# Graph convolution of one core's kernel: the gathered messages split into three bf16 parts, and a 0/1 one-hot in place of the weighted fp32 one

## The chip, the core and the metric

The kernel runs on one core of a Trainium2 chip. The metric is the device time of one launch in microseconds (us); the median of three runs before the change is 5700.91 us (5697.95 to 5701.5). Engines are named as in the profile: PE is TensorE's matmul, PEld its weight load, DVE VectorE, ACT ScalarE, POOL GpSimd, SP SyncE.

## The reference

The program is a chain of nine stages on a node matrix `x` of 625 nodes by 512 features; each stage works on a layer-normed `x` and most add their output to it. 20000 directed edges (`src`, `dst`, `edge_weight`), sorted by `dst`, join the nodes. The change touches the fourth stage alone, the graph convolution:

```python
deg  = segment_sum(w, dst_f) + self loops;  dinv = where(deg > 0, rsqrt(deg), 0)
h    = x @ W_conv                                        # 625 x 128
agg  = segment_sum(h[src_f] * (dinv[src_f] * w * dinv[dst_f])[:, None], dst_f) + b_conv
out  = agg @ W_lin + b_lin                               # 625 x 512
```

All of it is fp32.

## The kernel before

`program` runs the stages one after the other, each in a block of its own: no engine begins a stage before all have left the one before, apart from the layer norm between them, which is a block too. So a stage's length adds to the launch's time as it is.

The stage `gcn` has the functions of five queues. Edges lie as 125 partitions by 160 columns (R = 125, ET = 160); step k takes column k, so each step handles 125 edges and there are 160 steps. In the loops one lap is 16 steps (SLOTS).

- SP loads the weights; after DVE has scaled `h` by `dinv`, it stores `h` to HBM as `gcn_h_rows` (L528).
- POOL issues one indirect DMA per step (L538), which gathers 125 rows of 128 fp32 from `gcn_h_rows` into slot `rows[:, i]` of 16. Before every fourth gather it waits for `idx_ready`, which DVE signals.
- DVE makes, per step, the weighted one-hot `hot` of 125 x 625 fp32 (L561: compare `iota_f` with `dstf`, times `w`), two buffers deep; it first waits until PE has finished with the buffer (`hot_used`). On every fourth step it copies the next four columns of indices (L575), eight steps ahead.
- PE waits for the gather and for the one-hot and multiplies: `rows` as stationary operand, `hot` as moving one, 500 columns into bank 0 (L616) and 125 into bank 1 (L618), all 160 steps accumulated in PSUM. An fp32 product shows as two MATMUL records.
- ACT takes one square root (L595) and does nothing in the loop.

After the loop PE closes the banks (L621), DVE copies them out (L579, L580), and PE multiplies by `W_lin` (L625 to L629).

Nothing orders the loop but these semaphores. Three other stages are of use for reading prices: the edge count before it (L198 to L227: one-hots of 125 x 625 bf16 made from the fp16 iota, and bf16 products of 512 and 116 columns); the relational sum (L1080 gathers, L1133 index copies, L1135 one-hots in fp16, L1162 the upper part on ACT, L1138 the lower part on DVE, both 512 wide, L1179 products); and the split ahead of the LSTM (L1397, L1323, L1401, L1328: ACT, DVE, ACT, DVE, 512 wide, from PSUM).

Of the kernel before, what the change touches and what calls it, by code (L numbers as in the profile page):

```python
# [6 lines left out]
F32 = mybir.dt.float32  # L7
F16 = mybir.dt.float16
BF16 = mybir.dt.bfloat16
U32 = mybir.dt.uint32  # L10
I32 = mybir.dt.int32
ACT = mybir.ActivationFunctionType
# [3 lines left out]
N = 625  # L16
D = 512
R = 125
# [3 lines left out]
ET = E // R  # L22
# [456 lines left out]
SLOTS = 16  # L479
# [4 lines left out]
def gcn(nc, ctx, B):  # L484

    I = B.I
    H = I["L1_gnn_W_conv"].shape[1]

    def sb(name, shape, dt):
        return here.enter_context(nc.sbuf_tensor(name, shape, dt))  # L490

    def sem(name):
        return nc.alloc_semaphore(name)

    (loaded, deg_step, root_done, rsqrt_step, h_done, h_scaled, h_stored, idx_kept, hot_ready,
     hot_used, agg_done, agg_kept, bias_ready, bias_done, out_done) = [sem("gcn_" + n) for n in (
         "loaded deg_step root_done rsqrt_step h_done h_scaled h_stored idx_kept hot_ready "
         "hot_used agg_done agg_kept bias_ready bias_done out_done").split()]
    gathered = [sem(f"gcn_gathered{i}") for i in range(SLOTS)]
    idx_ready = [sem(f"gcn_idx_ready{i}") for i in range(SLOTS // LOT)]  # L500
    h_dram = nc.dram_tensor("gcn_h_rows", (N, H), F32, kind="Internal").ap()
# [1 line left out]
    with ExitStack() as here:  # L503
# [10 lines left out]
        idx_all = sb("gcn_idx_all", [R, ET + AHEAD * LOT], I32)  # L514
        idx = sb("gcn_idx", [R, SLOTS], I32)
        rows = sb("gcn_rows", [R, SLOTS, H], F32)
        hot = sb("gcn_hot", [R, 2, N], F32)
        aggT = sb("gcn_aggT", [H, N], F32)
        block = here.enter_context(nc.Block())

        @block.sync
        def _(sp):
            sp.dma_start(wc[:], I["L1_gnn_W_conv"].rearrange("(c p) h -> p c h", p=128)).then_inc(loaded, 16)
            sp.dma_start(wl[:], I["L1_gnn_W_lin"]).then_inc(loaded, 16)
            sp.dma_start(bc[:], I["L1_gnn_b_conv"].rearrange("(h a) -> h a", a=1)).then_inc(loaded, 16)
            sp.dma_start(bl[:], I["L1_gnn_b_lin"].rearrange("(a d) -> a d", a=1)).then_inc(loaded, 16)
            sp.wait_ge(h_scaled, NT)
            sp.dma_start(h_dram.rearrange("(j p) h -> p j h", p=R), h[:]).then_inc(h_stored, 16)  # L528
# [14 lines left out]
        @block.vector  # L543
        def _(dve):
            nc.vector.memset(idx_all[:, ET:ET + AHEAD * LOT], 0).then_inc(idx_kept, 1)
            nc.vector.tensor_copy(idx_all[:, 0:ET], B.srci[:]).then_inc(idx_kept, 1)
            nc.vector.tensor_scalar(deg[:], B.wdeg[:], 1.0, None, ALU.add).then_inc(deg_step, 1)
            dve.wait_ge(deg_step, 1)
            nc.vector.tensor_scalar(has[:], deg[:], 0.0, None, ALU.is_gt).then_inc(deg_step, 1)
            nc.vector.tensor_scalar(deg[:], deg[:], 1e-30, None, ALU.max).then_inc(deg_step, 1)  # L550
            dve.wait_ge(root_done, 1)
            inverse_root(nc, dve, dinv[:], deg[:], root[:], rsqrt_step, 0)
            nc.vector.tensor_tensor(dinv[:], dinv[:], has[:], ALU.mult).then_inc(deg_step, 1)
            dve.wait_ge(deg_step, 4)
            for m in range(NT):
                dve.wait_ge(h_done, m + 1)
                nc.vector.tensor_scalar(h[:, m, :], B.bank[2 + m][0:R, 0:H], dinv[:, m:m + 1], None,
                                        ALU.mult).then_inc(h_scaled, 1)

            def hots(k, b):  # L560
                nc.vector.tensor_scalar(hot[:, b, :], B.iota_f[:], B.dstf[:, bass.ds(k, 1)],  # L561
                                        B.w[:, bass.ds(k, 1)], ALU.is_equal, ALU.mult).then_inc(hot_ready, 1)

            dve.wait_ge(idx_kept, 2)
            for i in range(AHEAD):
                nc.vector.tensor_copy(idx[:, i * LOT:(i + 1) * LOT], idx_all[:, i * LOT:(i + 1) * LOT]
                                      ).then_inc(idx_ready[i], 1)
            with dve.Fori(0, ET // SLOTS) as g:
                for i in range(SLOTS):
                    k = g * SLOTS + i  # L570
                    dve.wait_ge(hot_used, k + 1)
                    if i % LOT == 0:

                        at = (i + AHEAD * LOT) % SLOTS
                        nc.vector.tensor_copy(idx[:, at:at + LOT], idx_all[:, bass.ds(k + AHEAD * LOT, LOT)]  # L575
                                              ).then_inc(idx_ready[at // LOT], 1)
                    hots(k, i % 2)
            dve.wait_ge(agg_done, 1)
            nc.vector.tensor_copy(aggT[:, 0:500], B.bank[0][0:H, 0:500]).then_inc(agg_kept, 1)  # L579
            nc.vector.tensor_copy(aggT[:, 500:N], B.bank[1][0:H, 0:R]).then_inc(agg_kept, 1)  # L580
            nc.vector.tensor_scalar(bc_wide[:], B.ones[0:H, 0:R], bc[:, 0:1], None, ALU.mult).then_inc(bias_ready, 1)
            for m in range(NT):
                dve.wait_ge(out_done, m + 1)
                nc.vector.scalar_tensor_tensor(out=B.x[:, m, :], in0=B.bank[2 + m][0:R, :],
                                               scalar=dinv[:, m:m + 1], in1=B.x[:, m, :], op0=ALU.mult,
                                               op1=ALU.add).then_inc(deg_step, 1)
            dve.wait_ge(bias_done, 1)
            dve.wait_ge(deg_step, 4 + NT)
            for m in range(NT):
                nc.vector.tensor_tensor(B.x[:, m, :], B.x[:, m, :], B.bank[7][0:R, :], ALU.add)  # L590

        @block.scalar
        def _(act):
            act.wait_ge(deg_step, 3)
            nc.scalar.activation(root[:], deg[:], ACT.Sqrt).then_inc(root_done, 1)  # L595

        @block.tensor
        def _(pe):
            pe.wait_ge(loaded, 64)
            for m in range(NT):  # L600
                for c in range(KC):
                    last = nc.tensor.matmul(B.bank[2 + m][0:R, 0:H], xnT[:, c, m * R:(m + 1) * R], wc[:, c, :],
                                            start=(c == 0), stop=(c == KC - 1))
                last.then_inc(h_done, 1)
            for i in range(2):
                last = nc.tensor.matmul(B.bank[i][0:H, :], B.zero[:, 0:H], B.zero[:], start=True, stop=False)
            last.then_inc(hot_used, 2)
            pe.wait_ge(h_scaled, NT)
            for m in range(NT):
                o = B.bank[0][0:H, m * R:(m + 1) * R] if m < 4 else B.bank[1][0:H, 0:R]  # L610
                nc.tensor.matmul(o, h[:, m, :], B.ident[0:R, 0:R], start=False, stop=False)
            with pe.Fori(0, ET // SLOTS) as g:
                for i in range(SLOTS):
                    pe.wait_ge(gathered[i], (g + 1) * 16)
                    pe.wait_ge(hot_ready, g * SLOTS + i + 1)
                    nc.tensor.matmul(B.bank[0][0:H, 0:500], rows[:, i, :], hot[:, i % 2, 0:500], start=False,  # L616
                                     stop=False)
                    nc.tensor.matmul(B.bank[1][0:H, 0:R], rows[:, i, :], hot[:, i % 2, 500:N], start=False,  # L618
                                     stop=False).then_inc(hot_used, 1)
            for i in range(2):  # L620
                last = nc.tensor.matmul(B.bank[i][0:H, :], B.zero[:, 0:H], B.zero[:], start=False, stop=True)  # L621
            last.then_inc(agg_done, 1)
            pe.wait_ge(agg_kept, 2)
            for m in range(NT):
                nc.tensor.matmul(B.bank[2 + m][0:R, :], aggT[:, m * R:(m + 1) * R], wl[:], start=True, stop=True  # L625
                                 ).then_inc(out_done, 1)
            pe.wait_ge(bias_ready, 1)
            nc.tensor.matmul(B.bank[7][0:R, :], bc_wide[:], wl[:], start=True, stop=False)
            nc.tensor.matmul(B.bank[7][0:R, :], B.ones[0:1, 0:R], bl[:], start=False, stop=True  # L629
                             ).then_inc(bias_done, 1)  # L630
# [1839 lines left out]
```

## Time and profile before

| what | value |
|---|---|
| median of 3 runs | 5700.91 us (5697.95 to 5701.5) |
| the profiled execution's own time | 5706.91 us |
| its span, first to last instruction | 5705.1 us |
| mean granted TensorE clock | 0.954 |
| PE busy | 5027.5 us (88%) |
| DVE busy | 2837.5 us (50%) |
| ACT busy | 1437.0 us (25%) |
| POOL busy | 633.6 us (11%) |
| the gcn loop, first gather to last product | 657.3 to 911.8 us |

Busy shares are an average over nine stages with different limits; for this change only the stretch from 657 to 920 us counts. Times in rows are us from the start of the span, or ns where a group's mean is given. A step's place in the loop is best read from the gathers, of which there is exactly one per step.

### The profile page before, as it was taken

The page shows a single profiled execution, that of the slowest core. Times are in us where ns is not written, and L with a number is a line of the kernel's source. Part 1 is how long each engine was busy: PE and PEld are TensorE (multiplying, and loading weights), DVE is VectorE, ACT ScalarE, POOL GpSimd, SP SyncE. Part 2 cuts the span into 40 slices and gives each one's busy share as a digit, 9 for nine tenths or more (in the row PEclk, how much of TensorE's full clock was granted, in tenths as well). Part 3 has the DMA queues.
Part 4 walks back from the last instruction along what each step waited for, and adds up shares of the span by engine and source line. Part 5 has one row for each costly group of instructions (what it writes and reads, how often), then busy time and mean ns, then how long its engine had stood idle before and what let it go on. Part 6 is the DMA issues. An engine that isn't in the chain of part 4 may idle for free. (4 is left out here: it accounts for less than half of the span.)

```text
span 5705.1 us, 267215 instructions
## 1 busy us (share of the span) xinstructions
PE 5027.5 (88%) x109528; PEld 3080.5 (54%) x109528; DVE 2837.5 (50%) x11506; ACT 1437.0 (25%) x4745; POOL 633.6 (11%) x1073
## 2 busy tenths in 40 slices
PE   8899686899998989999999999999999999777688
PEld 6644343444565446666666666666666666554444
DVE  4501344232554755555555555555555555574533
ACT  0000000012332343333333333333333333242222
POOL 0000382000662110000000000000000000021000
PEclk9899897999999989999999999999999999898877
DMA  0000111166444740000000000000000000000200
GB/s 11 15 30 15 30 42 31 56 240 240 125 120 144 258 129 12 10 10 12 10 10 10 12 10 10 12 11 10 10 12 10 10 12 10 19 15 36 74 12 9
DMA packets 157671, 265.00 MB, mean 46 GB/s; under 512 B 48686, under 2 KB 83636, under 8 KB 153241
## 3 DMA queue, kind: packets, MB, share of 16 engines
q1 hardware_dynamic: 102548, 181.63, 9.6%
q0 software_dynamic: 55040, 82.30, 5.1%
q8 instruction: 47, 0.77, 0.1%
q14 instruction: 36, 0.29, 0.0%
HBM read 178.38 MB, written 85.14 MB: 46 GB/s over the span
## 5 line engine op out<-in xcount | busy, mean ns | idle before, releaser
L1558 PE MATMUL bank<-lstm_w,step_h_parts 128*32 128x128 f16 x87360 | 1453.8, 220 | 241.8 <-issue 241.8
L1558 PEld LDWEIGHTS bank<-lstm_w,step_h_parts 128*32 128x32 f16 x87360 | 1238.4, 97 | 613.3 <-issue 349.3
L1629 DVE TRANSPOSE_TENSOR_REDUCE step_summed<-bank 128x4 f32 (+1 forms) x2500 | 792.4, 317 | 1085.2 <-PE bank L1558 914.5
L1553 PE MATMUL bank<-step_xg,step_rows 128*128 (+1 forms) x2500 | 757.7, 385 | 45.1 <-DMA step_xg<-lstm_xg 18.8
L1526 ACT ACTIVATE step_act_out<-step_summed,lstm_inv_scale 128x4 f32<-128x4 f32 x625 | 185.8, 297 | 1724.1 <-DVE step_summed L1629 1724.1
L1514 POOL COPY xnT<-step_state 128x4 f32 (+1 forms) x625 | 116.7, 187 | 2759.9 <-DVE step_state L1654 2759.9
L1179 PE MATMUL bank<-sum_parts,sum_hot 125*125 125x512 f16 x1600 | 346.9, 380 | 6.7 <-DVE sum_parts L1138 6.7
L1179 PEld LDWEIGHTS bank<-sum_parts,sum_hot 125*125 125x125 f16 x1600 | 219.0, 137 | 135.0 <-DVE sum_parts L1138 7.5
L1429 PE MATMUL bank<-xg_w,xnT 128*125 128x512 f32 x640 | 276.6, 595 | 6.7 <-DMA xg_w<-in_c_w_ih 6.7
L538 POOL DMA_INDIRECT gcn_rows<-gcn_h_rows,gcn_idx x160 | 202.5, 1265 | 703.3 <-issue 703.3
L1553 PEld LDWEIGHTS bank<-step_xg,step_rows 128*128 128x128 bf16 x2500 | 142.5, 97 | 167.7 <-issue 129.8
L1080 POOL DMA_INDIRECT sum_rows<-rel_h,sum_idx x160 | 211.7, 1323 | 118.0 <-DVE sum_idx L1133 80.0
L226 PE MATMUL bank<-cnt_hot_s,cnt_hot_d 125*125 125x512 bf16 x800 | 221.5, 387 | 3.4 <-DVE cnt_hot_s L202 3.4
L616 PE MATMUL bank<-gcn_hot,gcn_rows 125*128 125x500 f32 x320 | 177.7, 637 | 47.3 <-DMA gcn_rows<-gcn_h_rows,gcn_idx 44.5
L1588 PE MATMUL bank<-lstm_wsel,step_state 128*1 128x4 f32 x4992 | 215.0, 168 | 4.3
L1585 PEld LDWEIGHTS bank<-step_input_score,ones 1*1 1x1 f32 x1248 | 65.5, 75 | 281.8 <-issue 281.8
L1592 PE MATMUL bank<-step_h_weight,step_tc 128*1 128x4 f32 x4992 | 214.1, 168 | 0.0
L1532 ACT ACTIVATE step_act_out<-step_summed,lstm_inv_scale 128x4 f32<-128x4 f32 x625 | 185.9, 297 | 96.4 <-DVE step_summed L1629 26.0
L1429 PEld LDWEIGHTS bank<-xg_w,xnT 128*125 128x125 f32 x640 | 120.7, 189 | 162.1 <-issue 154.8
L143 ACT ACTIVATE ln_root<-ln_var_sb 125x5 f32<-125x5 f32 x8 | 1.7, 208 | 817.3 <-DVE ln_var_sb L124 817.3
L1529 ACT ACTIVATE step_act_out<-step_summed,lstm_inv_scale 128x4 f32<-128x4 f32 x625 | 185.8, 297 | 76.2 <-DVE step_summed L1629 16.6
L1537 ACT ACTIVATE step_act_out<-step_summed,lstm_inv_scale 128x4 f32<-128x4 f32 x625 | 185.9, 297 | 42.8 <-DVE step_summed L1629 1.5
(370 smaller groups left out, 6369.6 us busy)
## 6 DMA issues: line engine op xcount, KB each, us to landing
rel_h<-rel_h_sb SPq DMA_DIRECT2D x39, 1024.0 KB, 6.4
lstm_xg<-cnt POOLq DMA_DIRECT2D x80, 375.0 KB, 3.7
step_xg<-lstm_xg SPq DMA_DIRECT2D x375, 80.0 KB
xg_w<-in_c_w_ih SPq DMA_DIRECT2D x16, 1024.0 KB
lstm_w<-in_c_w_hh SPq DMA_DIRECT2D x16, 1024.0 KB, 11.6
cheb_w<-in_L_gnn_weight SPq DMA_DIRECT2D x8, 1024.0 KB
choose_we<-in_L_ffn_experts SPq DMA_DIRECT2D x8, 1024.0 KB
rel_bases<-in_L_gnn_bases SPq DMA_DIRECT2D x8, 1024.0 KB, 11.4
```

Source lines behind the costliest of these rows:

```text
L226: nc.tensor.matmul(B.bank[m][0:R, :], hd, hot_s[:, b, 0:512], start=False, stop=False)
L538: nc.gpsimd.indirect_dma_start(out=rows[:, i, :], out_offset=None, in_=h_dram, in_offset=bass.IndirectOffsetOnAxis(ap=idx[:, i:i + 1], axis=0)
L1080: nc.gpsimd.indirect_dma_start(out=rows[:, i, :], out_offset=None, in_=B.rel_h, in_offset=bass.IndirectOffsetOnAxis(ap=idx[:, i:i + 1], ax ...
L1179: last = nc.tensor.matmul(B.bank[m][0:R, :], hot[:, i % BUFS, m * R:(m + 1) * R], parts[:, i % BUFS, a, :], start=False, stop=False)
L1429: last = nc.tensor.matmul(B.bank[i % 6][0:R, :], xnT[:, c, m * R:(m + 1) * R], w[:, n % 2, c, :], start=(c == 0), stop=(c == KC - 1))
L1532: nc.scalar.activation(act_out[:, 8:12], summed[:, 8:12], ACT.Sigmoid, scale=L.inv[:, 0:1]).then_inc(sig_i, 1)
L1537: nc.scalar.activation(act_out[:, 12:16], summed[:, 12:16], ACT.Sigmoid, scale=L.inv[:, 0:1]).then_inc(sig_o, 1)
L1553: return nc.tensor.matmul(bank[:], rows[:, p, :], xg[:, at, :], start=True, stop=stop)
L1558: last = nc.tensor.matmul(bank[32 * q:32 * q + 32, 128 * s:128 * s + 128], h_parts[:, c, :], w[:, s, c, q, a, 128 * p:128 * p + 128], star ...
L1588: nc.tensor.matmul(score[:, 0:CELLS], state[:, k:k + 1], L.wsel[:, :, k], start=False, stop=False)
L1592: last = nc.tensor.matmul(score[:, 0:CELLS], tc[:, k:k + 1], h_weight[:, :, k], start=False, stop=(k == KC - 1))
L1629: nc.vector.tensor_reduce(summed[:, 4 * p:4 * p + 4], bank[:, bass.ds(s * 128, 128)].rearrange("p (b r) -> p b r", r=32), X_AXIS, ALU.add, ...
```

## The change

Each gathered message is multiplied by its edge weight and split into three bf16 numbers whose sum is the fp32 product: `hi` (ACT, bf16 of `w * row`), `rest` (DVE, `w * row - hi`, fp32), `mid` (ACT, bf16 of `rest`), `lo` (DVE, `rest - mid`, bf16). The one-hot holds only 0 and 1, in bf16, and comes from the fp16 iota. PE multiplies the three parts with the same one-hot: six bf16 products per step. The rings `hot`, `rest` and `parts` are four deep (`hot` was two deep), and PE waits for DVE's `hot_ready` and `lo_ready`; the wait for the gather moves from PE to ACT. POOL's and SP's programs stay as they are.

```diff
-        hot = sb("gcn_hot", [R, 2, N], F32)
+        hot = sb("gcn_hot", [R, 4, N], BF16)
+        rest = sb("gcn_rest", [R, 4, H], F32)
+        parts = sb("gcn_parts", [R, 4, 3, H], BF16)
...
-            def hots(k, b):
-                nc.vector.tensor_scalar(hot[:, b, :], B.iota_f[:], B.dstf[:, bass.ds(k, 1)],
-                                        B.w[:, bass.ds(k, 1)], ALU.is_equal, ALU.mult).then_inc(hot_ready, 1)
+            def split_rows(k, i):
+                dve.wait_ge(hi_ready, k + 1)
+                nc.vector.scalar_tensor_tensor(out=rest[:, i % 4, :], in0=rows[:, i, :], scalar=B.w[:, bass.ds(k, 1)],
+                                               in1=parts[:, i % 4, 0, :], op0=ALU.mult, op1=ALU.subtract
+                                               ).then_inc(rest_ready, 1)
+                nc.vector.tensor_scalar(hot[:, i % 4, :], B.iota_h[:], B.dstf[:, bass.ds(k, 1)], None,
+                                        ALU.is_equal).then_inc(hot_ready, 1)
+                dve.wait_ge(mid_ready, k + 1)
+                nc.vector.tensor_tensor(parts[:, i % 4, 2, :], rest[:, i % 4, :], parts[:, i % 4, 1, :], ALU.subtract
+                                        ).then_inc(lo_ready, 1)
...
-                    k = g * SLOTS + i
+                    k = dve.snap(g * SLOTS + i)
                     dve.wait_ge(hot_used, k + 1)
...
-                    hots(k, i % 2)
+                    split_rows(k, i)
...
             nc.scalar.activation(root[:], deg[:], ACT.Sqrt).then_inc(root_done, 1)
+            with act.Fori(0, ET // SLOTS) as g:
+                for i in range(SLOTS):
+                    k = act.snap(g * SLOTS + i)
+                    free = act.snap(k + 1)
+                    due = act.snap((g + 1) * 16)
+                    act.wait_ge(hot_used, free)
+                    act.wait_ge(gathered[i], due)
+                    nc.scalar.activation(parts[:, i % 4, 0, :], rows[:, i, :], ACT.Copy, scale=B.w[:, bass.ds(k, 1)]
+                                         ).then_inc(hi_ready, 1)
+                    act.wait_ge(rest_ready, free)
+                    nc.scalar.copy(parts[:, i % 4, 1, :], rest[:, i % 4, :]).then_inc(mid_ready, 1)
...
-            last.then_inc(hot_used, 2)
+            last.then_inc(hot_used, 4)
...
-                    pe.wait_ge(gathered[i], (g + 1) * 16)
                     pe.wait_ge(hot_ready, g * SLOTS + i + 1)
-                    nc.tensor.matmul(B.bank[0][0:H, 0:500], rows[:, i, :], hot[:, i % 2, 0:500], start=False,
-                                     stop=False)
-                    nc.tensor.matmul(B.bank[1][0:H, 0:R], rows[:, i, :], hot[:, i % 2, 500:N], start=False,
-                                     stop=False).then_inc(hot_used, 1)
+                    pe.wait_ge(lo_ready, g * SLOTS + i + 1)
+                    for a in range(3):
+                        nc.tensor.matmul(B.bank[0][0:H, 0:500], parts[:, i % 4, a, :], hot[:, i % 4, 0:500],
+                                         start=False, stop=False)
+                        last = nc.tensor.matmul(B.bank[1][0:H, 0:R], parts[:, i % 4, a, :], hot[:, i % 4, 500:N],
+                                                start=False, stop=False)
+                    last.then_inc(hot_used, 1)
```

## Rows read from the trace of the kernel before

**Rows 1.** Who waited for whom, 661 to 912 us: total us, times, longest
```profile
POOL gcn_rows L538 <- issue: 48.2, 158, 0.3
PE bank L616 <- DMA gcn_rows<-gcn_h_rows,gcn_idx: 44.5, 119, 8.6
```
**Rows 2.** Timeline, POOL's second gather and the last: start, duration, idle before
```profile
659.10 1.21 POOL L538 DMA_INDIRECT gcn_rows<-gcn_h_rows,gcn_idx  x1 [0.30 <-issue]
...
906.97 1.22 POOL L538 DMA_INDIRECT gcn_rows<-gcn_h_rows,gcn_idx  x1 [0.30 <-issue]
```
**Rows 3.** Timeline of PE, the loop's last product and the work behind it
```profile
910.52 1.10 PE L616 MATMUL bank<-gcn_hot,gcn_rows 125*128 125x500 f32 x2 [0.34 <-DMA gcn_rows<-gcn_h_rows,gcn_idx]
911.68 0.60 PE L621 MATMUL bank<-zero 128*128 128x512 bf16 x2
913.25 4.56 PE L625 MATMUL bank<-gcn_wl,gcn_aggT 128*125 128x512 f32 x10 [0.97 <-DVE gcn_aggT L580]
```
**Rows 4.** Timeline, POOL's gathers between 740 and 748 us
```profile
740.55 1.21 POOL L538 DMA_INDIRECT gcn_rows<-gcn_h_rows,gcn_idx  x1 [0.30 <-issue]
746.76 1.40 POOL L538 DMA_INDIRECT gcn_rows<-gcn_h_rows,gcn_idx  x1 [0.30 <-issue]
```
**Rows 5.** Timeline, DVE's one-hots beside the gathers of rows 4
```profile
741.15 0.89 DVE L561 TENSOR_SCALAR gcn_hot<-iota_f,dstf,w 125x625 f32<-125x625 f32 x1
747.20 0.61 DVE L561 TENSOR_SCALAR gcn_hot<-iota_f,dstf,w 125x625 f32<-125x625 f32 x1
```
**Rows 6.** Groups by line and shape, edge count, 20 to 242 us: busy us, mean ns
```profile
L226 PE MATMUL bank<-cnt_hot_s,cnt_hot_d 125*125 125x512 bf16 x800 | 221.5, 387 | 3.4 <-DVE cnt_hot_s L202 3.4
L198 DVE TENSOR_SCALAR cnt_hot_d<-iota_h,dstf 125x625 bf16<-125x625 f16 x159 | 61.5, 387 | 99.6 <-PE bank L227 99.6
```
**Rows 7.** Groups by line and shape, whole span, ACT and DVE: mean ns
```profile
L1162 ACT ACTIVATE sum_parts<-sum_rows,sum_norm 125x512 f16<-125x512 f32 x160 | 115.5, 722 | 243.1 <-PE bank L1179 219.5 <-DMA sum_rows<-rel_h,sum_idx 22.1 <-issue 1.4
L1535 ACT COPY step_input_score<-xn 1x4 f32 x622 | 109.6, 176 | 0.0
L1401 ACT CAST cnt<-xn 125x512 bf16<-125x512 f32 x80 | 49.1, 614 | 6.6 <-DVE xn L1323 6.4
L1932 ACT ACTIVATE gat_out<-gat_res 125x256 f32<-125x256 f32 x40 | 16.8, 419 | 7.2 <-DVE gat_res L2001 7.2
L2001 DVE SCALAR_TENSOR_TENSOR gat_res<-bank,gat_inv,gat_bias 125x256 f32<-125x256 f32 x40 | 19.4, 484 | 13.8 <-PE bank L1880 12.7
L1739 DVE SCALAR_TENSOR_TENSOR x<-bank,x 125x128 f32<-125x128 f32 x20 | 4.4, 284 | 1.8 <-PE bank L1729 1.7
```
**Rows 8.** Timeline of the relational sum, ACT's upper part and DVE's lower
```profile
1506.38 0.72 ACT L1162 ACTIVATE sum_parts<-sum_rows,sum_norm 125x512 f16<-125x512 f32 x1 [1.44 <-PE bank L1179]
1507.22 0.75 DVE L1138 SCALAR_TENSOR_TENSOR sum_parts<-sum_rows,sum_norm,sum_parts 125x512 f16<-125x512 f32 x1 [0.45 <-ACT sum_parts L1162]
```
**Rows 9.** Timeline of the relational sum: two gathers and the DVE work within them
```profile
1436.54 1.21 POOL L1080 DMA_INDIRECT sum_rows<-rel_h,sum_idx  x1 [0.30 <-issue]
1463.40 1.29 POOL L1080 DMA_INDIRECT sum_rows<-rel_h,sum_idx  x1 [0.30 <-issue]
...
1436.95 0.75 DVE L1138 SCALAR_TENSOR_TENSOR sum_parts<-sum_rows,sum_norm,sum_parts 125x512 f16<-125x512 f32 x1 [4.11 <-ACT sum_parts L1162]
1437.61 0.38 DVE L1135 TENSOR_SCALAR sum_hot<-iota_h,dstf 125x625 f16<-125x625 f16 x1
1463.23 0.39 DVE L1135 TENSOR_SCALAR sum_hot<-iota_h,dstf 125x625 f16<-125x625 f16 x1 [0.58 <-PE bank L1179]
```
**Rows 10.** Timeline of PE at the lower clock, edge count: successive products of one kind
```profile
21.25 0.64 PE L226 MATMUL bank<-cnt_hot_s,cnt_hot_d 125*125 125x512 bf16 x1
21.79 0.64 PE L226 MATMUL bank<-cnt_hot_s,cnt_hot_d 125*125 125x512 bf16 x1
```
**Rows 11.** Stretches: busy us (count) of each engine, then granted clock, DMA share, GB/s
```profile
946.00:997.00 51.00, 21.06 (x53) 11.35 (x54) 30.23 (x88) 0.00 (x0) 0.00 (x0) 0.60 0.00 0
661.00:911.70 250.70, 211.89 (x641) 109.32 (x642) 110.03 (x197) 0.00 (x0) 199.34 (x158) 0.99 0.17 41
```

More of the change, by code:

```diff
@@ L493, in sem @@
         return nc.alloc_semaphore(name)
[L495 to L498, printed above, removed]
+    (loaded, deg_step, root_done, rsqrt_step, h_done, h_scaled, h_stored, idx_kept, hi_ready, rest_ready,
+     mid_ready, lo_ready, hot_ready, hot_used, agg_done, agg_kept, bias_ready, bias_done, out_done) = [sem("gcn_" + n) for n in (
+         "loaded deg_step root_done rsqrt_step h_done h_scaled h_stored idx_kept hi_ready rest_ready "
+         "mid_ready lo_ready hot_ready hot_used agg_done agg_kept bias_ready bias_done out_done").split()]
     gathered = [sem(f"gcn_gathered{i}") for i in range(SLOTS)]
```

## The prediction

> **What bounds the kernel now.** The stages do not overlap, so the change is worth what it takes off or adds to the gcn stage, and the first question is who paces its loop. I read the waits of that stretch first, then POOL's and DVE's timelines side by side. The waits [rows 1] point away from PE: it waits 119 times of 160 for a gather that has not landed, 44.5 us in all. POOL is the only engine that waits for no other: before each of its 158 gathers there stand 0.3 us of its own issue and nothing else. The gathers run from 659.10 to 906.97 us, 158 of them [rows 2]: 247.87 / 158 = 1.569 us a step. A step of PE, by the stretch [rows 11], is 211.89 us / 160 = 1.32 us, so PE has 0.25 us spare per step. POOL's gather stream is the bound, and the fp32 products that the change replaces are not.
>
> The second reading is why a gather takes 1.21 us in one row and 1.40 in another [rows 4]. Laid beside DVE's one-hot [rows 5], with the phase counted from the gather's start: a one-hot that starts at 0.44 (747.20 - 746.76) lasts 0.61, ends at 1.05 and the gather takes 1.40, which is that end plus 0.35. One that starts at 0.60 (741.15 - 740.55) lasts 0.89 instead of 0.61, and the gather stays at 1.21. So the two engines exclude each other for a short part of the gather: whoever is late waits. By the first pair the gather suffers from a one-hot that has begun before it and ends after 1.21 - 0.35 = 0.86; by the second, a later one suffers itself, and the border between the two lies between 0.44 and 0.60. An undisturbed gather costs 1.21 + 0.30 = 1.515 us; the mean of 1.569 holds 0.054 us of this contention.
>
> **The change part by part.**
>
> *PE.* It loses two fp32 products a step and gets three pairs of bf16 ones, 500 and 125 columns. The edge count runs the same kind of pair (512 and 116 columns): 221.5 us of unbroken work over 800 pairs [rows 6] = 0.277 us a pair, so 0.83 us a step at the full clock. PE falls from 1.32 to 0.83 us and stays off the path; the gain of 0.49 us a step is worth nothing inside the loop, since the step before already waited for the gather.
>
> *ACT.* Two operations of 128 columns a step, none of which the trace has. For `hi` I take the line through a tiny copy (0.176) and L1162's 512 columns (0.722) [rows 7], which at 128 gives 0.31; I take 0.33, and the upper bound is the 256-column row, 0.42, the lower the tiny copy, 0.18. `mid` is a cast: between 0.176 and L1401's 0.614 the line gives 0.29, with bounds 0.18 and 0.42.
>
> *DVE.* `rest` and `lo` have two tensor inputs and 128 columns: 0.28 each by L1739; L2001 with 256 columns bounds it above at 0.48 [rows 7], and 0.18 below. The one-hot shrinks from 0.60 to 0.387 us [rows 6]. The index copies stay. DVE does 0.28 + 0.39 + 0.28 = 0.95 us a step, and the index copies that it has now.
>
> *Handoffs.* ACT's upper part ends at 1507.10 and DVE's lower part begins at 1507.22 [rows 8]: 0.12 us in a loop of the same kind. That is my price for each of the hand-offs; nothing to 0.2 bound it.
>
> *The new ring.* ACT and DVE take turns: `hi`, `rest`, `mid`, then ACT's next `hi`; `lo` and the one-hot lie beside. One turn is 0.33 + 0.12 + 0.28 + 0.12 + 0.29 + some 0.05 = 1.19 us. That is below 1.515, so the ring waits for gathers and not the other way. Behind ACT's waiting instruction stands only ACT's own next work; behind DVE's wait for `hi_ready` stand the one-hot, `lo` and, every fourth step, the index copy that feeds POOL. That copy is eight steps ahead of the gathers that it releases, 12 us at 1.515 a step, and a message now reaches PE 1.6 us after it lands, so POOL never waits for it. `hot_used` is four steps back, 6 us against a step's 2.4 us from landing to the last product: hidden too.
>
> *POOL.* Its instructions are the same; what changes is where DVE's port-holding operation falls. The last gather starts at 906.97 and its consumer at 910.52 [rows 2, 3]: 3.55 us, which is 0.52 after the start of the gather two later. From there `hi` ends at 0.85, `rest` runs 0.97 to 1.25, and the one-hot begins just before it ends (in [rows 9] 1437.61 against 1437.70), at about 1.17, and ends at 1.56, just into the next gather. The relational sum shows this very place: a one-hot that starts at 1.07 of the gather (1437.61 - 1436.54) lasts 0.38 and the gather takes 1.21. And even where the ring is quicker than I think, an operation of 0.39 us that begins before the lower border, 0.44, is over by 0.83: it has become too short to hold the gather up there. One place is left where it hurts: a one-hot that starts 0.17 ahead of a gather and ends 0.22 into it goes with a gather of 1.29 [rows 9]. So a gather costs 1.21 to 1.29; I take 1.21, the value at the place computed, which is 0.1 us from the bad one. If it drifts there, the longer gather moves the phase back by twice its excess, so it can't stay.
>
> Saved in the loop: (1.569 - 1.515) x 158 = 8.5 us; between 8.5 (1.21) and -4 (all at 1.29: 1.595).
>
> A rule of the Trainium skill bears on this. [rows 9] first: a DVE operation with two inputs in SBUF, 0.75 us long, lies from 0.41 to 1.16 within a gather of 1.21 us, and neither is lengthened. Its page SBUF — State Buffer, section "Who interferes with whom", says that a VectorE instruction with two SBUF inputs contends with a GpSimd instruction that reads SBUF, and that whichever starts second blocks fully. Were the gather such a reader, `rest` and `lo` would both stand in its way; the trace doesn't bear that out.
>
> *Around the loop.* The start is the same: the store of `h` and the first gather do not move. The end is longer: after the last landing stood one step of PE, 911.68 - 910.52 = 1.16 us [rows 3]. Now stand `hi` 0.33, `rest` 0.28, `mid` 0.29, `lo` 0.28 with four hand-offs of 0.12 at most, some 1.6, and then 0.83 of PE: 2.4 us, or 1.2 more. Bounds: 0.5 and 2.4 more.
>
> **Sum**, against the profiled execution of 5706.9 us: -8.5 + 1.2 = -7.3, 5699.6. The median of the runs stands 6.0 below that execution, so the same difference gives 5693.6 us there; I say 5694.
>
> **The rivals.**
>
> *A, the forecast:* gathers at 1.21 to 1.23, the loop about 242 us. 5694, own range 5690 to 5699. Chance 0.56.
>
> *B, nothing moves inside the loop.* The one-hot lands on the head of the next gather often enough that the pace stays 1.569; the tail remains. 5700.9 + 1.2 = 5702. For it: my phase is 0.1 us from that place and landings vary. Against: the phase corrects itself. 0.15.
>
> *C, the ring becomes the bound (slower).* Place: ACT's `hi` to `mid` to `hi`. With the upper bounds, 0.42 + 0.48 + 0.42 and three hand-offs of 0.12 with 0.05, it takes 1.73 us; it decides from 1.569 on. (1.73 - 1.569) x 158 + 1.2 = +27, 5728; at 1.65 +14. For it: three register values per step on ACT, for which no row gives a price. Against: 0.33 us of room. 0.11.
>
> *D, the clock falls.* PE's loop was at 0.99 with 85% busy; with 0.83 of 1.515 us it is 55% busy. The stretch from 946 us with 41% busy got 0.60 [rows 11]. At the lower level a pair takes 21.79 - 21.25 = 0.54 [rows 10], three 1.62 us: PE paces at 1.62, (1.62 - 1.569) x 158 = +8, and L625's products behind the loop, 4.56 us [rows 3], take up to as long again. All of the loop at 1.2 GHz: 5700.9 + 8 + 4.6 + 1 = 5715; a part of it, with the four-deep rings taking up the lag, only the tail's part, -7.3 + 4.6, 5698. As PE busy all of the time is also what brought the clock back, the part is more likely. 0.12, most of it within the band.
>
> *E, the quoted rule holds.* Every gather then waits out a two-input operation of 0.28 us: 1.515 + 0.28 = 1.795, (1.795 - 1.569) x 158 = +36, 5738. The measured row speaks against it. 0.04. The remaining 0.02 go to what I do not see.
>
> **How the numbers follow.** Two executions can't be told apart below about 0.2%, 11.4 us, so faster means under 5689.5 and slower over 5712.3. Even with every gather at 1.21 and the shortest tail the gain is 8.5 - 0.5 = 8 us: faster has 0.06, for an error in my floor. Slower takes C and E, 0.15. The rest, 0.79, is within. Range: A and B with the milder parts of C and D, 5688 to 5714.
>
> **What would show it.** Right: gathers nearly all at 1.21, pace 1.515; L561's successor at 0.39 with hardly any at 0.6 or more; PE waiting for DVE's `lo` each step; ACT waiting for the gather; about 0.83 us of PE a step; last gather to L621 5.9 us instead of 4.7. Wrong: POOL waiting for `gcn_idx`, which means that the ring paces (C); a clock of 0.5 in the loop (D); gathers of 1.3 and more (B by the one-hot, E by `rest` or `lo`). The forecast as a whole is wrong if the gathers' pace is not between 1.51 and 1.54.

## The result: 30 us slower, none of it in the changed stage

The changed kernel took 5731.7 us (median of 5 runs, 5722.28 to 5734.8), the kernel before 5701.5 (5697.95 to 5705.0): a ratio of 1.0051, 95% interval [1.0036, 1.0065]. The forecast was 5694, within 5688 to 5714. Two executions further below, one of e12 and one of the kernel before beside e15, ran at a granted clock of about 0.65, took over 7100 us and are left out.

The profile after has a span of 5732.9 us against 5705.1. Every layer norm has a square root on ACT, so the starts of these cut the span into stages. These are the four that matter, before and then after, in the timeline's columns (start, duration, engine, line, operation, operands, idle before):

```profile
632.39 0.21 ACT L143 ACTIVATE ln_root<-ln_var_sb 125x5 f32<-125x5 f32 x1 [2.40 <-DVE ln_var_sb L124]
927.41 0.21 ACT L143 ACTIVATE ln_root<-ln_var_sb 125x5 f32<-125x5 f32 x1 [287.13 <-DVE ln_var_sb L124]
1793.15 0.21 ACT L143 ACTIVATE ln_root<-ln_var_sb 125x5 f32<-125x5 f32 x1 [16.26 <-DVE ln_var_sb L124]
4974.11 0.21 ACT L143 ACTIVATE ln_root<-ln_var_sb 125x5 f32<-125x5 f32 x1 [2.78 <-DVE ln_var_sb L124]
```
```profile
632.88 0.21 ACT L143 ACTIVATE ln_root<-ln_var_sb 125x5 f32<-125x5 f32 x1 [2.40 <-DVE ln_var_sb L124]
926.53 0.21 ACT L143 ACTIVATE ln_root<-ln_var_sb 125x5 f32<-125x5 f32 x1 [17.04 <-DVE ln_var_sb L124]
1792.36 0.21 ACT L143 ACTIVATE ln_root<-ln_var_sb 125x5 f32<-125x5 f32 x1 [16.26 <-DVE ln_var_sb L124]
5005.65 0.21 ACT L143 ACTIVATE ln_root<-ln_var_sb 125x5 f32<-125x5 f32 x1 [2.40 <-DVE ln_var_sb L124]
```

The gcn stage, first row to second, went from 295.02 to 293.65 us. The stage from the third row to the fourth is the LSTM, 625 steps, no line of which was touched: from 3180.96 to 3213.29 us, +32.3. That is the whole loss. The other stages differ by less than 1 us, but for the one behind the LSTM, which went from 403.5 to 400.0; the kernel before, run again (e13), has 400.2 there too, so that is scatter.

**The gcn stage after**, where rows of it answer to [rows 1, 3, 6, 7]. First the waits (total us, times, longest), then the groups with busy us and mean ns:

```profile
PE bank L637 <- DVE gcn_parts L570: 102.1, 158, 10.3
ACT gcn_parts L615 <- DVE gcn_rest L564: 90.8, 160, 0.6
DVE gcn_rest L564 <- ACT gcn_parts L612: 89.0, 148, 10.2
ACT gcn_parts L612 <- DMA gcn_rows<-gcn_h_rows,gcn_idx: 62.0, 128, 20.6
POOL gcn_rows L540 <- issue: 44.8, 147, 0.3
POOL gcn_rows L540 <- DVE gcn_idx L584: 3.4, 11, 0.3
```
```profile
L540 POOL DMA_INDIRECT gcn_rows<-gcn_h_rows,gcn_idx x160 | 199.8, 1249 | 703.7 <-issue 700.4 <-DVE gcn_idx L584 3.4
...
L612 ACT ACTIVATE gcn_parts<-gcn_rows,w 125x128 bf16<-125x128 f32 x160 | 64.2, 401 | 66.1 <-DMA gcn_rows<-gcn_h_rows,gcn_idx 62.0 <-PE bank L639 1.2 <-issue 0.8
L567 DVE TENSOR_SCALAR gcn_hot<-iota_h,dstf 125x625 bf16<-125x625 f16 x160 | 61.0, 381 | 0.0
L564 DVE SCALAR_TENSOR_TENSOR gcn_rest<-gcn_rows,w,gcn_parts 125x128 f32<-125x128 f32 x160 | 56.2, 351 | 89.5 <-ACT gcn_parts L612 89.0 <-PE bank L639 0.5
L615 ACT CAST gcn_parts<-gcn_rest 125x128 bf16<-125x128 f32 x160 | 47.6, 298 | 90.8 <-DVE gcn_rest L564 90.8
...
L570 DVE TENSOR_TENSOR gcn_parts<-gcn_rest,gcn_parts 125x128 bf16<-125x128 f32 x160 | 46.8, 292 | 10.5
```

POOL is still the bound, as forecast, but its gathers take 1.249 us in the mean instead of 1.21. First gather to last is 1.554 us a gather, against 1.5705 before on the same measure; the forecast was 1.515.

**The LSTM step after.** One step on DVE, around the pick of the next cell, before and then after:

```profile
3001.41 0.15 DVE L1676 FIND_INDEX8 step_pick<-step_top,bank 1x8 uint32<-1x8 f32 x1
3002.98 0.32 DVE L1629 TRANSPOSE_TENSOR_REDUCE step_summed<-bank 128x4 f32 x1 [1.42 <-PE bank L1558]
```
```profile
3001.04 0.15 DVE L1698 FIND_INDEX8 step_pick<-step_top,bank 1x8 uint32<-1x8 f32 x1
3002.74 0.65 DVE L1651 TRANSPOSE_TENSOR_REDUCE step_summed<-bank 128x4 f32 x2 [1.54 <-PE bank L1580]
```

The idle time behind the pick grew from 1.42 to 1.54 us, and the profile puts it down to PE. But PE's products in the step stand where they stood (the 45th starts 1.344 us behind the pick before, 1.354 after, mean of 624 steps). DVE's own sequencer is what moved. Its instructions for the loop's head (the loop's line, DVEq is DVE's sequencer; times to 0.1 us), before and after, in the windows from these two picks on:

```profile
L1714 DVEq COMPARE_BRANCH  x1: 56/56/56, 3001.4 to 3001.4; - x1
L1714 DVEq MOVE  x1: 36/36/36, 3001.6 to 3001.6; - x1
```
```profile
L1736 DVEq COMPARE_BRANCH  x1: 56/56/56, 3001.1 to 3001.1; - x1
L1736 DVEq MOVE  x1: 36/36/36, 3001.4 to 3001.4; - x1
```

COMPARE_BRANCH is the back edge, the jump from the loop's last instruction to its first; MOVE is that first instruction. Averaged over the 623 back edges of the trace, as start less the start of the pick:

```
us behind the pick           before   after
back edge ends               0.065    0.065
head's MOVE                  0.200    0.342
load of the picked index     0.293    0.428
first semaphore instruction  0.969    1.111
last instruction ahead of the reduce ends  1.500  1.648
reduce (L1629 / L1651)       1.604    1.713
sigmoid f starts on ACT      1.956    2.064
third reduce                 2.475    2.527
mean step                    4.541    4.589
```

The jump back takes 0.142 us longer. Some of it falls into slack that DVE had against PE, 0.109 is left at the first reduce, and 0.048 at the end of the step (mean of the steps under 10 us; only the first step of the stage is longer). 0.048 x 624 = 30 us.

### The profile page after: what moved, and what is told of

Read it like the earlier page. It is cut to its first block and busy times, and to the rows that moved or that the text cites. A ratio compares the mean times of both kernels' runs of the same rounds, so it can differ in the third digit from the quotient of the medians.

```text
span 5732.9 us, 268800 instructions
## 1 busy us (share of the span) xinstructions
PE 4866.5 (85%) x109222; PEld 3045.5 (53%) x109848; DVE 2871.2 (50%) x11826; ACT 1523.7 (27%) x5065; POOL 630.4 (11%) x1073
## 5 line engine op out<-in xcount | busy, mean ns | idle before, releaser
L1651 DVE TRANSPOSE_TENSOR_REDUCE step_summed<-bank 128x4 f32 (+1 forms) x2500 | 769.2, 315 | 1073.4 <-PE bank L1580 981.4
L1575 PE MATMUL bank<-step_xg,step_rows 128*128 (+1 forms) x1876 | 617.8, 384 | 175.2 <-issue 155.4
L637 PE MATMUL bank<-gcn_hot,gcn_parts 125*128 125x500 bf16 x480 | 146.8, 375 | 102.1 <-DVE gcn_parts L570 102.1
L1184 ACT ACTIVATE sum_parts<-sum_rows,sum_norm 125x512 f16<-125x512 f32 x160 | 115.5, 722 | 244.9 <-PE bank L1201 223.9
```

The lines of the kernel that those rows point to most:

```text
L1575: return nc.tensor.matmul(bank[:], rows[:, p, :], xg[:, at, :], start=True, stop=stop)
L1651: nc.vector.tensor_reduce(summed[:, 4 * p:4 * p + 4], bank[:, bass.ds(s * 128, 128)].rearrange("p (b r) -> p b r", r=32), X_AXIS, ALU.add, ...
```

## The experiments

The change adds 62 instructions to DVE's stream ahead of the LSTM, 81 to PE's and 85 to ACT's. **Theory F:** these move DVE's LSTM loop in instruction memory to where its back edge is slow. **Rival G:** the shift of PE or ACT, or what the gcn stage leaves behind, does it. "Slot" is the place within a block of 256 instructions. The trace has 32 instructions of DVE from one MOVE to the COMPARE_BRANCH, so the loop is 32 long; the expectations below count 31. In the table, MOVE is the median time of the head's MOVE behind the pick, and a ratio is against runs of the kernel before made beside that run (their medians are 5700.4 to 5704.4), so ratios compare better than times.

```
run                           us  ratio [95%]             MOVE   step   LSTM    gcn stage
before                    5701.5                          0.200  4.541  3180.96  295.02
after                     5731.7  1.0051 [1.0036,1.0065]  0.342  4.589  3213.29  293.65
e1  before, DVE +62       5726.0  1.0038 [1.0025,1.0052]  0.335  4.577  3204.42  293.07
e2  before, PE/ACT shift  5713.4  1.0016 [1.0007,1.0025]  0.200  4.543  3185.15  302.34
e3  after, DVE +2         5735.0  1.0055 [1.0042,1.0069]  0.342  4.589  3211.26  292.56
e4  after, DVE +194       5705.3  1.0000 [0.9991,1.0009]  0.200  4.545  3184.31  293.53
e5  after, slot 0         5703.2  1.0003 [0.9994,1.0012]  0.200  4.545  3186.41  292.71
e6  after, slot 235       5719.8  1.0032 [1.0020,1.0045]  0.298  4.572  3200.96  292.81
e7  after, slot 110       5725.5  1.0039 [1.0026,1.0053]  0.342  4.590  3213.24  291.98
e8  after, slot 160       5702.8  1.0001 [0.9992,1.0010]  0.201  4.548  3188.01  292.92
e9  no one-hots, slot 40  5698.7  0.9995 [0.9986,1.0004]  0.200  4.540  3185.55  287.21
e10 one-hot first, slot 0 5695.5  0.9990 [0.9981,0.9999]  0.201  4.544  3184.76  286.58
e11 e10, PE at slot 0     5698.3  0.9997 [0.9988,1.0006]  0.201  4.539  3185.67  287.53
e12 before, slot 110      5724.0  1.0040 [1.0027,1.0053]  0.342  4.580  3206.42  294.57
e13 before again          5703.9  1.0004 [0.9995,1.0013]  0.200  4.541  3182.08  293.86
e14 before, all, slot 110 5732.2  1.0055 [1.0041,1.0069]  0.342  4.576  3204.04  301.39
e15 one-hot first, 110    5722.6  1.0032 [1.0019,1.0044]  0.342  4.582  3208.28  287.52
e16 one-hot first, as is  5701.3  0.9997 [0.9987,1.0006]  0.186  4.545  3186.48  287.90
```

**Is it the place of DVE's code?** e1 and e2 put the change's instruction counts into the kernel before, where the gcn stage has room:

```diff
             dve.wait_ge(deg_step, 4)
+            for _ in range(63):        # 62 instructions in the stream (3 and 195 give 2 and 194)
+                dve.engine_nop()
             for m in range(NT):
...
@@ e2 alone: waits that are already met, two to an instruction, in place of the above
+            for _ in range(168):
+                act.wait_ge(deg_step, 3)
...
+            for _ in range(162):
+                pe.wait_ge(loaded, 64)
```

> The kernel before, with 62 instructions that do nothing added to DVE's stream ahead of the gcn stage's transform (as many as the change adds to that stream), so that DVE's code of all later stages lies 62 instructions further on. Theory F (the change's loss is the place of DVE's LSTM loop in instruction memory): the LSTM stage goes from 3181 to about 3213 us, its step from 4.554 to 4.60 us, the span to about 5732 us, although no arithmetic differs; the gcn stage stays at 295 +-2 us. Rival G (the loss comes from the shift of PE's or ACT's streams, or from what the gcn stage leaves behind in the memories): the LSTM stage stays at 3181 us and the time at 5702.

> The kernel before, with 81 instructions added to PE's stream and 85 to ACT's in the gcn stage (waits that are already met), as many as the change adds to each, and none to DVE's. Theory F: the LSTM stage stays at 3181 us, the time at 5702 to 5708 (the added waits may cost up to 5 us at the head of the gcn stage). Rival G: LSTM stage about 3213 us, time about 5732 or more.

> The changed kernel with 2 more instructions that do nothing in DVE's stream, 64 more than before in all. Theory F has two forms. F1 (what counts is the place within a small line of a few instructions; 64 is a multiple of 4): LSTM stage back at 3181 us, time about 5700. F2 (what counts is the place within a large block): LSTM stage still about 3213 us, time 5732. Rival G: 5732.

> The changed kernel with 194 more instructions that do nothing in DVE's stream ahead of the gcn transform, 256 more than before in all. Theory F, in both forms: DVE's LSTM loop is back at its old place within a block of 256, the LSTM stage is 3181 us and the time about 5700 (the 194 instructions lie beside the wait for the weights and PE's products; at worst +5 us in the gcn stage). Rival G: LSTM stage 3213 us, time 5732.

F holds. Nothing but 62 empty instructions made the kernel before 22 us slower than its own runs beside it (5726.0 against 5704.0); its LSTM stage, 3204, is 9 us short of the 3213 that F gave, which is taken up below. The shifts of PE and ACT left the MOVE at 0.200 and the step within 2 ns; e2's 9 us (5713.4 against 5704.0 beside it) are mostly the added waits in the gcn stage (+7.3). A shift of 64 is still slow (e3), one of 256 as fast as none (e4), so it is the place within something larger than a few instructions.

**Which places are slow?** The head is placed by the loop itself:

```diff
-            with dve.Fori(1, STEPS - 1) as t:
+            with nc.Fori(1, STEPS - 1, engines=OrderedEngineSet([dve.engine]), head_slot={dve.engine: 0}) as t:
```

> The changed kernel with the head of DVE's LSTM loop (31 instructions) placed at slot 0 of a 256-instruction fetch block, whatever lies ahead of it. Theory B (a back edge is slow when the loop straddles the end of a 256-instruction block, and fast when it lies within one): step 4.554 us, the head's MOVE 0.20 us after the pick, LSTM stage 3181 to 3185 us, time about 5703. Rival A (what matters is some other alignment, or slots in the first half are fast and in the second slow): not told apart by this run alone, see the other three. Rival G (not the placement): 5732.

> The same with the head at slot 235, so that the loop's last 10 instructions lie in the next block of 256. Theory B: slow, the head's MOVE 0.34 us after the pick, step 4.60 us, LSTM stage about 3211 us, time about 5732. Rival A (a half of the block, or slots by themselves): fast or slow, but then slot 160 is the same as this one.

> The same with the head at slot 110, so that the loop straddles the middle of the block (slot 128) and no end. Theory B: fast, LSTM stage 3181 to 3185 us, time about 5703. Rival M (blocks of 128 instructions): slow as slot 235, LSTM stage about 3211 us.

> The same with the head at slot 160, the whole loop inside the second half of the block. Theory B: fast, LSTM stage 3181 to 3185 us, time about 5703. Rival A (the second half is slow): LSTM stage about 3211 us, time about 5732.

Theory B missed in one of four: slot 110 straddles no end of a 256-block, only its middle, and is the slowest place of all. Slot 235 is slow as it said, but by less (MOVE 0.298 instead of 0.34, stage 3201 instead of 3211); why less is not shown. Slots 0 and 160 are fast, slot 40 too (e9), though the loop straddles slot 64 there. The two places that were straddled and slow are 128 and 256: what must not be straddled is a multiple of 128. The group of DVE's reduce over 1800 to 4960 us (count, busy, mean ns, idle before), in e8 and then in e7:

```profile
L1652 DVE TRANSPOSE_TENSOR_REDUCE step_summed<-bank 128x4 f32 (+1 forms) x2496 | 790.5, 317 | 1079.3 <-PE bank L1581 914.1 <-PE bank L1576 8.7
```
```profile
L1652 DVE TRANSPOSE_TENSOR_REDUCE step_summed<-bank 128x4 f32 (+1 forms) x2480 | 763.3, 315 | 1056.6 <-PE bank L1581 965.8 <-PE bank L1576 8.6
```

The time "waited for PE" at L1581 is 52 us longer in e7, over four steps fewer, though PE's 45th product starts 1.34 us behind the pick in both. All idle time before the reduces is 23 us shorter: the first reduce of a step comes 0.09 us later, and the other three then wait 0.02 to 0.06 us less each. So the name behind an idle time says little here.

Is it a fetch? The page of the profile counts DMA packets that carry instructions, by queue (packets, MB, share); the kernel before:

```profile
q8 instruction: 47, 0.77, 0.1%
q14 instruction: 36, 0.29, 0.0%
```

From 2160 to 4940 us, with some 600 back edges, there is not one such packet before, after or in e7. So the 0.14 us of each jump is not a fetch by DMA; what the sequencer does in it stays open. A packet of q14 has half the bytes of one of q8 (0.29 / 36 against 0.77 / 47), which would fit a unit of 128 instructions beside one of 256; that q14 serves DVE is not shown. A fetch does show once: the first back edge of the stage took 2.9 to 3.0 us with the head at slot 0 or 40 (e5, e9, e10), and an instruction packet starts 1.1 us behind that pick.

The Trainium skill, page Runtime: NRT & Kernel Launch, section "Instruction fetch mechanics", has blocks of 256 instructions, two of them held, and a stall for a jump out of these two. These runs agree that where the target lies decides what a taken branch costs. They differ in the size, 128 in place of 256, and in the condition, since a loop of 32 instructions never leaves two neighbouring blocks; the runs decide.

**Does the place alone make all of it, and what scatters?**

e12 and e15 are that edit with `head_slot={dve.engine: 110}`, e13 has no edit, and e14 is e12 with e2's waits and `spare = [sem(f"gcn_spare{i}") for i in range(4)]`.

> The kernel before, with nothing of the gcn change, and the head of DVE's LSTM loop at slot 110, so that it straddles slot 128. If the place alone makes the whole loss: head's MOVE 0.342 us after the pick, LSTM stage 3209 to 3213 us, time about 5731, ratio 1.005. If a part of the loss needs the changed kernel as well (the 62 instructions in the kernel before gave 3204 us, not 3213): LSTM stage 3204 us, time 5725, ratio 1.004.

> The kernel before, unchanged, with a second profile. The LSTM stage of the changed kernels whose loop lies well is 3184 to 3188 us, and 3181 us in the one profile of the kernel before. If it differs by as much between two executions of one kernel: 3184 to 3188 us here. If the 3 to 5 us belong to the changed kernels: 3181 us again. Ratio 1.000.

> The kernel before with DVE's LSTM loop at slot 110, and with 81 met waits more in PE's stream, 85 in ACT's and four unused semaphores, as many as the change adds to each. The badly placed variants of the kernel before have steps of 4.577 to 4.580 us, those of the changed kernel 4.588 to 4.590, and only the latter have DVE's first semaphore instruction of the step 12 ns later against what stands ahead of it. If the lengths of the other streams make that: step 4.588 us, LSTM stage 3211 to 3213 us. If something else that the changed kernel leaves behind makes it: 4.579 us and 3206 us, and it stays open. gcn stage 301 to 302 us from the waits added at its head.

> The variant with the one-hot first, with DVE's LSTM loop badly placed, head at slot 110. Its well placed form has DVE's first semaphore instruction of a step 82 ns behind what stands ahead of it, like the kernels before; the changed kernel and its other variants have 95. If these 13 ns are what adds 7 us to a badly placed changed kernel: 82 ns, LSTM stage 3204 to 3206 us, time about 5717. If the 7 us come from something else in the changed kernels: LSTM stage 3211 to 3213 us, time about 5724.

Without the change, slot 110 gives 3206.4 us: 24 to 25 of the 32 us are the place alone. The rest, 5 to 9 us, sits in the badly placed changed kernels (step 4.589, 4.589, 4.590), not in the badly placed kernels before (4.577, 4.580, 4.576). It goes with a second detail of DVE's sequencer: from the end of the instruction ahead of it to the step's first semaphore instruction are 82 ns in every kernel before and 95 in the changed kernel and e3 to e9. Other streams' lengths and semaphore numbers don't make it (e14 has them, and 82). The four kernels with the one-hot first have 82 as well, and badly placed (e15) a step of 4.582 and a stage 5 us shorter than e7's. So the 13 ns go with most of that rest. That they cause it is not shown: e15's stage, 3208.3, lies between the two ranges that its expectation set (3204 to 3206 and 3211 to 3213), and it differs from e7 in the order of the gcn loop too. **What makes them 95 stays open.** Where the place is good they cost nothing that shows: steps of 4.540 to 4.548 with 95, 4.539 to 4.545 with 82 and the one-hot first, 4.541 to 4.543 in the kernels before. The kernel before shows the LSTM stage 1.1 us apart in its two executions; the well placed changed kernels, of either kind, have 2 to 7 us more than these, and so has e2 (3 to 4). That is not explained.

**Why did the gathers not come down to 1.21?** The timeline of the changed kernel, five gathers and what DVE and ACT do beside them:

```profile
740.18 0.38 DVE L567 TENSOR_SCALAR gcn_hot<-iota_h,dstf 125x625 bf16<-125x625 f16 x1
740.36 1.28 POOL L540 DMA_INDIRECT gcn_rows<-gcn_h_rows,gcn_idx  x1 [0.30 <-issue]
...
741.95 1.21 POOL L540 DMA_INDIRECT gcn_rows<-gcn_h_rows,gcn_idx  x1 [0.30 <-issue]
742.04 0.29 DVE L570 TENSOR_TENSOR gcn_parts<-gcn_rest,gcn_parts 125x128 bf16<-125x128 f32 x1
742.34 0.40 ACT L612 ACTIVATE gcn_parts<-gcn_rows,w 125x128 bf16<-125x128 f32 x1 [0.33 <-DMA gcn_rows<-gcn_h_rows,gcn_idx]
742.87 0.35 DVE L564 SCALAR_TENSOR_TENSOR gcn_rest<-gcn_rows,w,gcn_parts 125x128 f32<-125x128 f32 x1 [0.45 <-ACT gcn_parts L612]
743.14 0.38 DVE L567 TENSOR_SCALAR gcn_hot<-iota_h,dstf 125x625 bf16<-125x625 f16 x1
743.46 1.21 POOL L540 DMA_INDIRECT gcn_rows<-gcn_h_rows,gcn_idx  x1 [0.30 <-issue]
743.98 0.40 ACT L612 ACTIVATE gcn_parts<-gcn_rows,w 125x128 bf16<-125x128 f32 x1 [0.42 <-DMA gcn_rows<-gcn_h_rows,gcn_idx]
744.85 0.38 DVE L567 TENSOR_SCALAR gcn_hot<-iota_h,dstf 125x625 bf16<-125x625 f16 x1
744.97 1.34 POOL L540 DMA_INDIRECT gcn_rows<-gcn_h_rows,gcn_idx  x1 [0.30 <-issue]
...
746.48 0.38 DVE L567 TENSOR_SCALAR gcn_hot<-iota_h,dstf 125x625 bf16<-125x625 f16 x1
746.62 1.32 POOL L540 DMA_INDIRECT gcn_rows<-gcn_h_rows,gcn_idx  x1 [0.30 <-issue]
```

One-hots that end 0.06, 0.20, 0.24 and 0.26 us into a gather go with gathers of 1.21, 1.28, 1.32 and 1.34: a gather that starts under a DVE operation takes 1.08 plus what is left of it, where that is 0.13 to 0.30. 84 gathers keep to this within 0.013; seven with 0.32 to 0.37 left took 1.21, which is not explained. An operation with two inputs does it as well: three third parts (L570) with 0.23 to 0.24 left go with gathers of 1.31 to 1.33.

68 of the 160 took 1.24 or more, the first gather and 67 of this kind. The kernel before has 78, but by the other way, which the prediction read from [rows 4, 5]: in 76 of them a one-hot that began 0.29 to 0.46 into the gather was still running at 0.89, and the gather ended 0.34 behind it.

Theory P says that the one-hot over the start is what makes the changed kernel's long gathers. e9 makes four one-hots ahead of the loop and none in it, so its sums are not the reference's; e10 moves them to where no gather starts:

```diff
             def split_rows(k, i):
+                nc.vector.tensor_scalar(hot[:, i % 4, :], B.iota_h[:], ..., ALU.is_equal).then_inc(hot_ready, 1)
                 dve.wait_ge(hi_ready, k + 1)
                 nc.vector.scalar_tensor_tensor(out=rest[:, i % 4, :], ...).then_inc(rest_ready, 1)
-                nc.vector.tensor_scalar(hot[:, i % 4, :], B.iota_h[:], ..., ALU.is_equal).then_inc(hot_ready, 1)
                 dve.wait_ge(mid_ready, k + 1)
```

> The changed kernel with the gcn loop's one-hots left out: four are made once before the loop and PE reads those (so the sum goes to wrong rows); and, for the stage far behind, DVE's LSTM loop with its head at slot 40, so that it straddles slot 64. gcn stage: theory P (a gather that starts while a DVE operation is running waits for its end, and the one-hot, which runs from 0.3 us before the gather's start to 0.1 to 0.26 us behind it, is the one that does it) gives gathers of 1.21 us mean in place of 1.249, a pace of 1.515 us in place of 1.553, and a stage shorter by 6 us. Rival Q (the long gathers are the gather's own): 1.249 and 1.553 us stay. LSTM stage: if the line is 128 slots, fast, 3181 to 3188 us; if it is 64 or fewer, slow, 3200 to 3213 us.

> The changed kernel with DVE's LSTM loop at slot 0 and, in the gcn loop, the one-hot put ahead of the wait for the high part in place of behind the second part. Theory P: the one-hot follows the third part of the tile before, at 0.4 to 0.8 us behind a gather's start, where it covers no start; gathers 1.22 us mean, pace 1.53 us, gcn stage 3 to 4 us shorter than in the changed kernel. If the one-hot is itself held until 0.9 us behind the start, the second part moves later by 0.3 us and covers the next start: pace 1.55 to 1.60. Rival Q: pace 1.553. Time 5699 with the first, 5703 with Q.

e11 adds `head_slot={pe.engine: 0}` to PE's loop, e16 is e10 with the loop as it was.

> As the run before, and PE's LSTM loop (1090 instructions) too with its head at slot 0. If PE's own place costs anything (its 44th product of a step came 8 ns later where PE's stream was moved by 81 instructions), the LSTM stage is 3181 us in place of 3186; if not, the same within 2 us.

> The same with the one-hot first and the loop where it falls, 50 instructions further on than in the kernel before. By the runs so far the kernel before has its head between positions 36 and 65 of a 128-slot line; so it is slow (LSTM stage 3204 to 3213 us, time 5717 to 5724) if that head is at 48 or later, and fast (3182 to 3186 us, time 5695) if it is earlier.

Theory P holds, and e10 does better than the 1.22 and 1.53 expected of it. Without one-hots the gathers take 1.214 us (pace 1.519); with them first, 1.211 (pace 1.516, 2 of 160 over 1.24), with nothing left out. The timeline of e10:

```profile
739.15 1.21 POOL L541 DMA_INDIRECT gcn_rows<-gcn_h_rows,gcn_idx  x1 [0.30 <-issue]
739.80 0.69 DVE L564 TENSOR_SCALAR gcn_hot<-iota_h,dstf 125x625 bf16<-125x625 f16 x1
740.41 0.33 DVE L567 SCALAR_TENSOR_TENSOR gcn_rest<-gcn_rows,w,gcn_parts 125x128 f32<-125x128 f32 x1
740.67 1.21 POOL L541 DMA_INDIRECT gcn_rows<-gcn_h_rows,gcn_idx  x1 [0.30 <-issue]
```

The one-hot now starts 0.65 into a gather and is itself held, 0.69 us long instead of 0.38; it ends at 1.34, ahead of the next gather (136 of the 160 do so, at 1.33 to 1.36). It pays on DVE, which has the time, and no longer on POOL. The second part (L567) ends 0.07 into the next gather, under the 0.13 that costs.

e10 takes 5695.5 us, ratio 0.9990 [0.9981, 0.9999]: 36 us below the changed kernel, and 6 below the one before, inside the band that the prediction called no change. That it beats the kernel before is only just clear, and e11 and e16, with the same gcn code, have 0.9997 with 1 inside the interval. Its gcn stages (e10, e11, e15, e16: 287.4 in the mean) are 6.7 us shorter than those of the kernels before (before, e1, e12, e13: 294.1). PE's place gives nothing (e11). e16 is where luck put the loop well, as it did in the kernel before; by e1 and e16, and a loop of 32, the head of the kernel before lies between 35 and 46 of its 128 (62 more straddles the end, 50 more doesn't).

## Why the prediction was wrong, step by step

- **The step that failed** is its first sentence: "The stages do not overlap, so the change is worth what it takes off or adds to the gcn stage". The stages do not overlap, but the step from there to the worth of the change put a term at nothing: what 62 instructions more in DVE's stream do to the stages behind. They moved DVE's LSTM loop across a multiple of 128, and its stage grew by 32.3 us (24 to 25 of them by the place alone, e12), while the gcn stage changed by -1.4. No rival had this; it fell in the 0.02 for what I did not see. With the loop well placed (e4, e5) the changed kernel takes 5705 and 5703, inside the range but at B's time, not at the forecast's 5694.
- *POOL is the bound, PE is not:* right. The pace followed only the gathers.
- *The gather costs 1.21 at the place computed:* wrong in size. The reading of the kernel before holds (76 of its 78 long gathers, above), and so does that an operation this short no longer does that harm. The one-hot was put at 1.17 to 1.56 of the gather, ending 0.05 into the next; 743.14 in the rows above is that case. But the high part took 0.401 instead of 0.33, the second part 0.351 instead of 0.28, and landings vary (ACT starts the high part at 0.39 of a gather in one row, 0.52 in the other). That reached the 0.1 us that I had named as the distance to the bad place. "It can't stay" there was wrong too: it is there in 67 gathers of 160. First gather to last fell by 2.7 us (249.71 to 247.02) instead of 8.5: between A and B, nearer to B.
- *DVE's and ACT's operations:* mid 0.298 (0.29), lo 0.292 (0.28), one-hot 0.381 (0.387) as said.
- *PE 0.83 us a step:* 0.81, three pairs that follow each other by 0.27. *The clock:* granted 0.99 over 661 to 906 us, so D did not come.
- *The ring at 1.19 us:* about 1.41 (0.40 + 0.20 + 0.35 + 0.03 + 0.30 + 0.13 up to the next high part, by the timeline). Still under the pace, so C did not come, but with half the room I gave it. *POOL never waits for the index copy:* 11 times, 3.4 us in all, not visible in its gaps.
- *The tail, +1.2:* the last gather starts at 904.67 and the zero product at 911.00, 6.33 us; before it was 4.71 [rows 2, 3]. +1.6. To the stage's end it is 21.86 against 20.44, +1.4.
- *E, the quoted rule of the Trainium skill* (SBUF — State Buffer, "Who interferes with whom"): the trace after doesn't bear it out either. The third part at 742.04, with two inputs in SBUF, lies within a gather (741.95 to 743.16) that took 1.21. Over a gather's start such an operation does hold it (three times, above), but so does the one-hot, with one input.

Together: -2.7 + 1.4 and -0.1 ahead of the first gather give the stage's -1.4; the forecast had -7.3, and with the one-hot moved the stage has -6.7 (e10, e11, e15, e16).

## What to carry to other kernels

A change can be paid for in a stage that it does not touch: compare the stages first, all of them, and when an unchanged loop is longer, look at the engine's sequencer rows behind the back edge before believing the engine that the wait is put down to. A short loop that runs hundreds of times on the critical path should have its head pinned, here so that its 32 instructions do not straddle a multiple of 128. And where an engine's gathers set the pace, ask of every operation on DVE whether a gather will start under it; here, moving it within the step cost nothing (e10).

## What the runs showed of the hardware that was not expected

- DVE's back edge to the first instruction of the loop: 0.135 us from the branch's end where the loop straddles no multiple of 128 instructions (e4, e8), 0.277 where it straddles 128 from slot 110 (e7, e12), 0.233 where it straddles 256 from slot 235 (e6). At the place of e16 it was 0.121. No instruction packet is moved in the some 600 jumps of before, after and e7 between 2160 and 4940 us.
- A gather on POOL is held in two ways: by a DVE operation over its start, to 1.08 us plus the remainder (0.13 to 0.30 us, 84 gathers after), and by one that began ahead of 0.46 and runs past 0.89 of it, to 0.34 us behind that one's end (76 gathers before). A bf16 one-hot that starts 0.64 to 0.92 into a gather is held itself, until 1.34 (e10).
- A semaphore instruction on DVE is issued 82 or 95 ns behind the same predecessor, the same throughout one kernel, by something that no run here found.
